# A graph layer with attention and a two-of-eight expert block: input and attention added during the gather, one normalized tensor, double-buffered slot tables

## What is computed

```python
xn = _layernorm(x, axis=-1)
# graph part, _L0_gnn_ref: h = xn @ W, every node also linked to itself
deg = segment_sum(w_cnt, fdst); dinv = rsqrt(deg)
gnn = segment_sum((dinv[fsrc] * dinv[fdst] * w_cnt)[:, None] * h[fdst], fsrc)
# attention part, _L0_mix_ref: linear attention, 8 heads, feature map elu + 1
kv = einsum('blhd,blhe->bhde', k, v); k_sum = sum(k, axis=1)
mix = (einsum('blhd,bhde->blhe', q, kv) / normalizer[..., None]) @ wo + bo
x = x + gnn + mix
# expert part, _L0_ffn_ref, on xt = _layernorm(x): two of eight experts per token
logits = xt @ Wr + br                      # top 2, weights from their softmax
xe = layernorm(xt) * ln_g[e] + ln_b[e]     # a second normalization of xt
y = gelu(xe @ W1[e] + b1[e]) @ W2[e] + b2[e]
x = x + sum over the two experts of weight * y
```

## Time and profile before

| | us |
|---|---|
| median of 3 runs (2602.28 to 2605.21) | 2603.84 |
| the profiled execution's own time | 2604.59 |
| its span | 2602.7 |

### The profile page before, as it was taken

The page is one execution under the profiler, slowest core; times in us unless marked ns, Lnnn a source line. Parts: engine busy times, 40 slices in busy tenths (PEclk is TensorE's granted clock), DMA queues, the critical chain, the costliest instruction groups (busy, mean ns, idle before and its releaser), DMA issues.

```text
span 2602.7 us, 56074 instructions
## 1 busy us (share of the span) xinstructions
PE 2180.6 (84%) x12041; PEld 1796.9 (69%) x12042; DVE 1328.7 (51%) x2437; ACT 1200.7 (46%) x3274; POOL 1324.0 (51%) x1388
## 2 busy tenths in 40 slices
PE   0999994888888888888888866658999999999990
PEld 0677773666666666666666645517999999999980
DVE  8799996565666666666666546651111111111116
ACT  2444441666666666666666644502333333333320
POOL 6766565677777777777777761002222222222220
PEclk9999997899999999999999997558999999999995
DMA  4000003333333333333333494434555555555539
GB/s 135 1 1 1 1 1 112 93 105 105 104 104 105 105 105 105 105 105 105 105 104 104 122 80 69 132 124 137 180 180 180 181 179 182 181 180 181 181 108 297
DMA packets 139535, 304.96 MB, mean 117 GB/s; under 512 B 29056, under 2 KB 77101, under 8 KB 139376
## 3 DMA queue, kind: packets, MB, share of 16 engines
q0 software_dynamic: 59232, 143.39, 21.9%
q1 hardware_dynamic: 80272, 161.23, 17.4%
HBM read 270.55 MB, written 33.98 MB: 117 GB/s over the span
## 4 chain that ended last, share of the span: by engine, by line
PE 57%; DMA 20%; DVE 9%; issue 5%; DVEq 4%; POOL 3%; ACT 0%; SPq 0%; ACTq 0%; POOLq 0%
PE B L1403 18%; DMA BIG<-table,W2A 18%; PE B L1499 15%; PE B L1508 14%; DVEq L665 3%; DVE BIG L660 3%; PE B L1392 2%; PE B L1465 1%; POOL BIG L507 1%; PE B L1309 1%; PE B L1342 1%; DVE W1A L1061 1%; POOL W2A L483 1%; PE B L1487 1%; PE B L1326 1%
## 5 line engine op out<-in xcount | busy, mean ns | idle before, releaser
L507 POOL DMA_INDIRECT BIG<-table,W2A x880 | 834.5, 948 | 301.3 <-issue 202.4
L547 DVE TENSOR_TENSOR ACC<-ACC,B 128x512 f32 x880 | 605.4, 688 | 451.9 <-PE B L1403 312.3
L1403 PE MATMUL B<-BIG 128*128 128x256 f32 x1760 | 429.8, 388 | 83.9 <-DMA BIG<-table,W2A 81.7
L1403 PE MATMUL B<-BIG,W2A 128*128 128x256 f32 x1760 | 427.6, 386 | 85.9 <-DMA BIG<-table,W2A 85.8
L1079 ACT ACTIVATE BIG<-B,SMALL 128x128 f32<-128x128 f32 (+1 forms) x889 | 251.1, 387 | 506.3 <-PE B L1499 506.3
L1403 PEld LDWEIGHTS B<-BIG 128*128 128x128 f32 x1760 | 322.4, 191 | 182.9 <-issue 143.6
L1403 PEld LDWEIGHTS B<-BIG,W2A 128*128 128x128 f32 x1760 | 316.8, 190 | 174.3 <-issue 137.2
L1499 PEld LDWEIGHTS B<-BIG,W1A 128*128 128x128 f32 x3360 | 393.6, 193 | 7.9 <-DVE BIG L550 2.6
L1499 PE MATMUL B<-BIG,W1A 128*128 128x128 f32 x3360 | 394.4, 276 | 2.0 <-DVE BIG L550 2.0
L1508 PE MATMUL B<-W2A,BIG 128*128 x1680 | 380.1, 379 | 0.7 <-DVE ACC L547 0.7
L1508 PEld LDWEIGHTS B<-W2A,BIG 128*128 128x128 f32 x1680 | 311.0, 190 | 39.1 <-issue 1.1
(11 more groups left out here) (208 smaller groups left out, 2203.8 us busy)
## 6 DMA issues: line engine op xcount, KB each, us to landing
W1A<-in_w SPq DMA_DIRECT2D x105, 1024.0 KB, 5.1
BIG<-table,W2A POOLq DMA_INDIRECT x880, 2.8
W2A<-in_w SPq DMA_DIRECT2D x1, 8192.0 KB, 30.1
table<-ACC SPq DMA_DIRECT2D x7, 896.0 KB, 7.1
token_x<-BIG SPq DMA_DIRECT2D x49, 128.0 KB, 1.7
W2A<-in_x SPq DMA_DIRECT2D x1, 6144.0 KB
W1A<-pick_y SPq DMA_DIRECT2D x4, 896.0 KB, 10.8
W2A<-pick_y SPq DMA_DIRECT2D x4, 896.0 KB, 11.2
```

Source lines behind the costliest of these rows:

```text
L507: pool.indirect_dma_start(G[h][:, u, :], None, table, bass.IndirectOffsetOnAxis(ap=idx_s[h][:, u:u + 1], axis=0)).then_inc(gath[h][u // 2] ...
L547: return dve.tensor_tensor(o, a, b, op)
L1403: last = mm(B[u][:, k * D:(k + 1) * D], OH[h % 2][:, u, k * P:(k + 1) * P], G[h][:, u, :], start=True, stop=True)
```

## The change

Three things change.

- **Gather loop.** The residual is no longer formed after the loop. `add_attention` adds the attention output, times `sdeg` (the root of the degree, 1 / dinv), to acc itself, and a new `add_inputs`, after the third batch of a step, adds xr times sdeg to acc. Both stand behind a `drain`, since the adds around them may touch the same tile. acc thus holds the residual divided by dinv.
- **Router.** Tiles go in four groups (6, 10, 16 and 17 tiles), unrolled. From the variance of acc come one root over two columns and one scale: ACT writes only the twice normalized tensor xs2, in pairs of tiles. PE transposes that one, ACT evicts a pair at once, and the logits are corrected by `unscale`. Stores go in pairs. The 8 MB load follows the last store. ACT scales acc by dinv, 49 operations, after its last eviction. Router weights are loaded at about 440 us.
- **Slot tables.** `pc_tile` and `pc_tokens` have two buffers; one of the four table operations moves to ACT; DVE waits for PE two groups back, before its first operation.

```diff
-RG = 7
-RSLOT = [u % 4 for u in range(RG)]
-RLAG = [next(k for k in range(1, RG + 1) if RSLOT[u - k] == RSLOT[u]) for u in range(RG)]
+LGROUPS = [range(a, b) for a, b in zip((0, 6, 16, 32), (6, 16, 32, NT))]
+NPAIR = (NT + 1) // 2
...
-        pc_tile = grid(BIG, 2688, ST, PC, BF16)
-        pc_tokens = grid(BIG, 3424, 2 * ST, PC, BF16)
+        pc_tile = [grid(BIG, 2688 + 736 * s, ST, PC, BF16) for s in range(2)]
+        pc_tokens = [grid(W1A, R0 + 8 * NE + 1472 * s, 2 * ST, PC, BF16) for s in range(2)]
...
+            sp.dma_start(wr_s, wr.rearrange("(k p) e -> p k e", p=P)).then_inc(router_in, 16)
+            sp.dma_start(br_s, br.to_broadcast([P, E])).then_inc(router_in, 16)
...
-            sp.dma_start(wr_s, wr.rearrange("(k p) e -> p k e", p=P)).then_inc(router_in, 16)
...
-            sp.wait_ge(x_done, 1)
...
+            for j in range(NPAIR):
+                n = min(2, NT - 2 * j)
+                sp.wait_ge(xs_ready, 2 * j + n)
+                sp.dma_start(token_x[2 * j * P:(2 * j + n) * P, :].rearrange("(t p) d -> p t d", p=P), xs2[j % 4][:, 0:n, :]
+                             ).then_inc(xs_out[j % 4], 16)
...
+            ch.add(dve.tensor_copy(sdeg, col[12][:, 0:NT]))
+            ch.add(tt(dinv2, dinv, dinv, ALU.mult))
...
             def add_attention(t):
+                dve.drain()
                 when(dve, tk_v, q_out, t + 1)
+                a = acc[:, bass.ds(t, 1), :].rearrange("p o d -> p (o d)")
+                dve.scalar_tensor_tensor(out=a, in0=B[7][:, 0:D], scalar=sdeg[:, bass.ds(t, 1)], in1=a,
+                                         op0=ALU.mult, op1=ALU.add).then_inc(q_added, 1)
+
+            def add_inputs(t):
+
+                dve.drain()
+                a = acc[:, bass.ds(t, 1), :].rearrange("p o d -> p (o d)")
                 xt = xr[:, bass.ds(t, 1), :].rearrange("p o d -> p (o d)")
-                tt(xt, xt, B[7][:, 0:D], ALU.add).then_inc(q_added, 1)
+                dve.scalar_tensor_tensor(out=a, in0=xt, scalar=sdeg[:, bass.ds(t, 1)], in1=a, op0=ALU.mult, op1=ALU.add)
 
...
                 add_sums(i * BATCHES + 2)
+                if not isinstance(i, int) or i < NT:
+                    add_inputs(i)
...
+            dve.wait_ge(table_out, 16 * TPARTS)
...
-            def residual(t):
...
-            group(NT // RG - 1, True)
...
+            def statistics(g):
+                for t in g:
+                    dve.bn_stats(stats2[:, t:t + 1, :], acc[:, t:t + 1, :])
+                dve.drain()
+
...
+            def variances(g):
...
+                tt(var, var, dinv2[:, part], ALU.mult)
+                dve.drain()
+                ts(stat_in[:, 1, part], var, LN_EPS, ALU.add)
+                ts(stat_in[:, 0, part], var, 1.0 + LN_EPS, ALU.mult, LN_EPS * LN_EPS, ALU.add)
+                dve.drain()
+                dve.sem_inc(std_in, 1)
+
+            def scales(k, g):
+
+                part = slice(g.start, g.stop)
+                dve.wait_ge(std_out, k + 3)
+                dve.reciprocal(rstd2[:, part], stat_root[:, 0, part])
+                dve.drain()
+                tt(rstd2[:, part], rstd2[:, part], dinv[:, part], ALU.mult)
+                dve.drain()
+                dve.scalar_tensor_tensor(out=nmr2[:, part], in0=small(18)[:, part], scalar=-0.5, in1=rstd2[:, part],
+                                         op0=ALU.mult, op1=ALU.mult)
+                dve.drain()
+                dve.sem_inc(norm2_ready, 1)
+
+            statistics(LGROUPS[0])
+            variances(LGROUPS[0])
+            for k, g in enumerate(LGROUPS):
+                if k + 1 < len(LGROUPS):
+                    statistics(LGROUPS[k + 1])
+                scales(k, g)
+                if k + 1 < len(LGROUPS):
+                    variances(LGROUPS[k + 1])
...
+            ch.link(dve.reciprocal(unscale, stat_root[:, 1, 0:NT]))
+            ch.link(tt(unscale, unscale, stat_root[:, 0, 0:NT], ALU.mult))
...
+            ch.link(tt(logits, B[4][:, 0:NE].rearrange("p (t e) -> p t e", e=E), unscale.unsqueeze(2).to_broadcast(full), ALU.mult))
+            ch.link(tt(logits, logits, br_s.unsqueeze(1).to_broadcast(full), ALU.add))
...
+                when(dve, tk_v, pc_used, g - 1)
                 tt(pc_at[s], pc_digits, cols(slot_at, P), ALU.is_equal)
-                tt(pc_tile, pc_digits[:, 0:ST, :], cols(slot_tile, ST), ALU.is_equal)
-                dve.drain()
-                when(dve, tk_v, pc_used, g)
-                tt(pc_tokens[:, 0:ST, :], pc_tile, cols(pick_col, ST), ALU.mult)
-                ts(pc_tokens[:, ST:2 * ST, :], pc_tile, row_1, ALU.mult)
+                tt(pc_tile[s], pc_digits[:, 0:ST, :], cols(slot_tile, ST), ALU.is_equal)
                 dve.drain()
                 dve.sem_inc(pc_ready, 1)
+                tt(pc_tokens[s][:, 0:ST, :], pc_tile[s], cols(pick_col, ST), ALU.mult)
+                dve.drain()
+                dve.sem_inc(pc_ready, 1)
 
             dve.wait_ge(slot_e_out, 16)
-            slot_digits(0, 0)
-            with dve.Fori(0, PICKS // PC // 2) as i:
-                slot_digits(i * 2 + 1, 1)
-                slot_digits(i * 2 + 2, 0)
+            for g in range(PICKS // PC):
+                slot_digits(g, g % 2)
...
+            dve.wait_ge(res_ready, 1)
...
-            def transposed_x2(g, u):
...
-            norm_group(NT // RG - 1, True)
...
+            def transposed_x2(j):
+
+                n = min(2, NT - 2 * j)
+                act.wait_ge(x2T_ps, j + 1)
+                if j >= 4:
+                    act.wait_ge(logit_ps, 2 * (j - 4) + 2)
+                cp(x2T[j % 4][:, 0:n * KD, :], B[j % 4][:, 0:n * D].rearrange("p (g n) -> p g n", n=P)).then_inc(x2T_ready, 1)
+
+            def roots(k):
+
+                part = slice(LGROUPS[k].start, LGROUPS[k].stop)
+                act.wait_ge(std_in, k + 3)
+                cp(stat_root[:, :, part], stat_in[:, :, part], ACT.Sqrt).then_inc(std_out, 1)
+
+            roots(0)
+            for k, g in enumerate(LGROUPS):
+                act.wait_ge(norm2_ready, k + 1)
+                for t in g:
+                    j = t // 2
+                    if t % 2 == 0 and j >= 4:
+                        act.wait_ge(x2T_ps, j - 3)
+                        act.wait_ge(xs_out[j % 4], 16 * (j // 4))
+                    cp(xs2[j % 4][:, t % 2, :], acc[:, t, :], ACT.Identity, scale=rstd2[:, t:t + 1], bias=nmr2[:, t:t + 1]
+                       ).then_inc(xs_ready, 1)
+                    if t % 2 == 1 and t >= 3:
+                        transposed_x2(t // 2 - 1)
+                    if t == g.stop - 3 and k + 1 < len(LGROUPS):
+                        roots(k + 1)
+            transposed_x2(NPAIR - 2)
+            transposed_x2(NPAIR - 1)
+            for t in range(NT):
+                last = cp(acc[:, t, :], acc[:, t, :], scale=dinv[:, t:t + 1])
+            last.then_inc(res_ready, 1)
...
+            for g in range(PICKS // PC):
+                act.wait_ge(pc_ready, 2 * g + 1)
+                if g >= 2:
+                    act.wait_ge(pc_used, g - 1)
+                cp(pc_tokens[g % 2][:, ST:2 * ST, :], pc_tile[g % 2], scale=row_1).then_inc(pc_rows, 1)
...
-            def transpose_x2(t, u):
...
-            route_group(NT // RG - 1, True)
...
+            def transpose_x2(j):
+                n = min(2, NT - 2 * j)
+                pe.wait_ge(xs_ready, 2 * j + n)
+                if j >= 4:
+                    pe.wait_ge(x2T_ready, j - 3)
+                for k in range(n * KD):
+                    last = nc.tensor.transpose(B[j % 4][:, k * P:(k + 1) * P], xs2[j % 4][:, k // KD, k % KD * P:(k % KD + 1) * P], ident)
                 last.then_inc(x2T_ps, 1)
 
-            def route_group(g, last_group=False):
-                for u in range(RG):
-                    t, r = g * RG + u, RSLOT[u]
-                    if not last_group or u + 2 < RG:
-                        transpose_x2(t + 2, (u + 2) % RG)
-                    if u % 2 == 0:
-                        when(pe, tk_t, x2T_even, g * ((RG + 1) // 2) + u // 2 + 1)
-                    else:
-                        when(pe, tk_t, x2T_odd, g * (RG // 2) + u // 2 + 1)
+            def router_product(j):
+                pe.wait_ge(x2T_ready, j + 1)
+                for t in range(2 * j, min(2 * j + 2, NT)):
                     for k in range(KD):
-                        last = mm(B[4][:, bass.ds(t * E, E)], x2T[r][:, k, :], wr_s[:, k, :], start=k == 0, stop=k == KD - 1)
+                        last = mm(B[4][:, t * E:(t + 1) * E], x2T[j % 4][:, t % 2 * KD + k, :], wr_s[:, k, :],
+                                  start=k == 0, stop=k == KD - 1)
                     last.then_inc(logit_ps, 1)
 
-            transpose_x2(0, 0)
-            transpose_x2(1, 1)
-            with pe.Fori(0, NT // RG - 1) as g:
-                route_group(g)
-            route_group(NT // RG - 1, True)
+            transpose_x2(0)
+            for j in range(NPAIR):
+                if j + 1 < NPAIR:
```

(45 more changed lines are left out.)

112 lines of the change are left out of this document (17 added, 95 removed).

## The result

The changed kernel takes 2620.81 us (median of 5 executions, 2619.17 to 2621.70) against 2604.77 before: ratio 1.0064, 95% interval 1.0048 to 1.0079. One of the five executions of before took 10714.63 us and is left out of the ratio; the other four took 2602.28 to 2605.21. The forecast was 2612.5 us, slower, with a range of 2580 to 2632. The profiled execution took 2620.16 us, 15.6 more than the one of before.

What follows compares the result with a forecast made beforehand. POOL was taken to bound the gather loop and handoff chains the two stages after; DVE's added work would outgrow its slack. 2604.59 + 42.6 + 0.2 - 23.4 - 10.8 = 2613.2, stated as 2612.5 us, range 2580 to 2632.

Steps and rivals of the forecast that it cites:

- a floor of 19.33 us: Gather loop before the change: the least DVE time for one step, summed from start to start of its instructions.
- the slack of 0.72: Gather loop before the change: DVE's room per step, in us, against POOL's 20.05 us.
- 19.33 + 1.79 = 21.12: Gather loop: DVE's step in us with both new drained operations, 1.07 over POOL, in steps 1 to 48.
- +42.8: Start to T0: forecast lengthening in us, with 42.6 from the gather loop's excess over POOL.
- the backlog: Gather loop: DVE can fall 8.8 us behind before POOL stands still, so that much does not move T0.
- 49 x 1.17 = 57.4: Router: PE is the bound at 1.17 us a tile, 57.4 us for 49 tiles, from T0 + 9.5.
- The wait for the second group: Router: about 2.5 us where PE has used up six tiles and DVE still has sixteen statistics before the second group's scales.
- T0: End of the last gather add, 1589.5 us in the run before; forecast near 1632 after the change.
- the scalings on ACT: After the router: 49 residual scalings, about 0.5 us each, hidden by 5 us before ACT's row copies are wanted.
- -10.8: Slot tables: PE runs group after group at 5.5 us instead of 7.36, so the stage takes 10.8 us less.
- The clock as a rival: Slot groups, perhaps router: PE's clock rises, giving 2596.6 us, or 2578 if in the router too; chance 0.20.
- The cover of the loop: Gather loop: the two operations add at most 0.72 us per step, T0 stays, 2569.8 us; chance 0.15.

Runs made afterwards that it cites:

- e4: The kernel before with only a drain added ahead of the attention add: 2601.93 us, ratio 1.0003.
- e3: The changed kernel with attention added undrained to the input's tile, and both added to acc one step later in one drained operation: 2574.12 us, ratio 0.9894.
- e1: The kernel before with the new gather loop alone, keeping its old router and slot tables: 2650.99 us, ratio 1.0193.
- e7: e2 with 36 wide f32 products on PE, read by nobody, ahead of the slot groups: ratio 0.9886 to the kernel before.
- e11: e2 with the slot tables' second operand laid out row by row, read side by side by PE, written apart: ratio 0.9952 to the kernel before.
- e8: e2 with unread wide f32 products on PE, 70 ahead of the router and four behind each pair of tiles: ratio 0.9859 to the kernel before.
- e2: The changed kernel with attention added undrained to the input's tile and the 49 input additions made in steps 50 to 54: 2565.92 us, ratio 0.9868.

## Why the prediction was right

Against the sum of 2613.2 the profiled execution came 7.0 us later. The loop makes 7.7 of them, the router 1.9, the slot tables take back 1.7 and the rest 0.9. The mechanism held in all three stages; that the misses behind the loop nearly cancel is luck.

**The loop.** Right in its mechanism: start-to-start times of DVE, a floor of 19.33 us, POOL at 20.05, the slack of 0.72. e4 and e3 put the two operations at 0.75 and 0.92 us each (20.08 and 20.25 less 19.33), where the prediction had 0.79 and 1.00. Mis-sized is the step, "19.33 + 1.79 = 21.12": it is 21.30. Of the 0.18 the start of the attention add makes 0.07 (1.12, put at 1.05) and the add ahead of the division 0.11 (1.16, put at 1.05); the input add starts after 1.00, as put. With both operations in the loop three starts in a step come some 0.1 us later than with one: attention add 1.12 (1.01 in e4), input add 1.00 (0.90 in e3), the add ahead of the division 1.16 (1.05). It is so in e1 as well. 48 x 0.18 = 8.6 us cover the gap of 7.7 between the forecast +42.8 and +50.5; most of the rest went into the backlog, which was put at 8.8 us and comes out as 48 x (21.30 - 20.05) - 50.5 = 9.5. What delays these starts stays open: no run tried it.

**The router.** Mechanism right, PE bound at 1.2 GHz. The term "49 x 1.17 = 57.4" is too small: a pair takes 2.45, not 2.35, and PE works for 60.7 us in all. The wait for the second group, put at 2.5, is 1.54, so 2.3 us of the 3.3 remain. Logits at T0 + 71.8 (69.4 forecast), weight load out at T0 + 66.4 (64.4), slot_experts landed at T0 + 97.7 (95.6): each some 2 us late by these two terms. DVE's chain from logits to slot tables took 25.7 (25.9), and the scalings on ACT were hidden, by 9 us where 5 were put: they took 0.40 us each, not 0.5.

**The slot tables.** Groups end to end, 5.34 us each where 5.5 was put: -12.5 for -10.8.

**The clock as a rival** did not come true in either place; the windows of after read 0.50 from the first transposes to the last slot product. It was wrong in its price too: it took the slot products to be limited by the clock, and e7 and e11 show that they were not. The Trainium skill, page "TensorE: Matmul & The Clock Gate", Part 1, says that sustained matmul activity releases the clock; 37.4 us of products without a gap did not here, so measurement and page differ, and the measurement decides. Its Part 4 says that the high clock does not engage for transposes; the router's row of 0.50 agrees. In e8, with the clock at 1.00, transposes and narrow products ran about twice as fast all the same: the four transposes of a pair took 0.44 us in place of 0.88, the eight narrow instructions 0.81 in place of 1.57. On e11 the Trainium skill, page "SBUF — State Buffer", section "Door 1: The DMA port swizzle", puts the stride that costs nothing at eight bf16 elements; e11 agrees: 14 apart they cost a factor of two.

**The cover of the loop** as a rival was the right question: e2 shows that its 2570 (0.987 of before) was to be had, by putting the additions where adds wait, in the last five steps.

## What to carry to other kernels

An engine that looks half idle by busy time can have no slack at all: add up start-to-start times of its instructions over one step, drains and registers included, and compare with the pace of the engine that leads. A small operation behind a drain costs most of its price in its start (halving its width took 0.13 us off it, a second start cost 0.55), so put it where the loop waits anyway (here the last steps, where DVE waited for PE) or do several behind one drain. A PE that is busy without a gap is not thereby at its rate: compare the time of one product with its columns before blaming the clock.
